# A two-layer decoder on one core: the expert mixture of a batch moves half an iteration forward

## The reference

```python
h = silu(einsum('td,eid->eti', xt, W1)) * einsum('td,eid->eti', xt, W3)
y = einsum('etd,te->td', einsum('eti,edi->etd', h, W2), combine)
```

## Time and profile before

| | us |
|---|---|
| median of 3 runs | 695.19 (691.85 to 702.54) |
| the profiled execution, its own time | 692.92 |
| its span | 691.0 |
| PE busy in the span | 538.9 (78%) |
| DVE busy | 412.9 (60%) |
| ACT busy | 298.5 (43%) |
| POOL busy | 124.3 (18%) |

### The profile page before, as it was taken

One profiled execution on the slowest core, in us unless ns is written; L12 is line 12 of the kernel. 1 busy time (PEld: TensorE's weight loads), 2 busy tenths in 40 slices (PEclk: granted clock), 3 DMA queues, 4 the chain that ended last, 5 costly groups with the idle time before them and its releaser, 6 DMA issues.

```text
span 691.0 us, 10909 instructions
## 1 busy us (share of the span) xinstructions
PE 538.9 (78%) x4385; PEld 379.9 (55%) x4412; DVE 412.9 (60%) x993; ACT 298.5 (43%) x470; POOL 124.3 (18%) x162
## 2 busy tenths in 40 slices
PE   2566627737999898998989999899998957846765
PEld 1323414415677575776767778677775734524433
DVE  3567794785446754457555573436644583573786
ACT  2314314605671136621377214763158617622443
POOL 2246052430000320000023000220003000211343
PEclk9977866967999899999999999999999997986989
DMA  6035011301000010000001000010020000000000
GB/s 212 0 142 216 25 48 48 96 9 52 1 1 2 0 62 1 2 1 1 0 2 62 1 1 1 1 63 1 1 87 6 1 0 1 1 1 0 16 16 31
DMA packets 5405, 20.98 MB, mean 30 GB/s; under 512 B 843, under 2 KB 3019, under 8 KB 4460
## 3 DMA queue, kind: packets, MB, share of 16 engines
q1 hardware_dynamic: 5356, 20.30, 8.4%
HBM read 19.25 MB, written 1.05 MB: 29 GB/s over the span
## 4 chain that ended last, share of the span: by engine, by line
PE 59%; DVE 27%; ACT 7%; issue 5%; DMA 1%; POOL 0%; SPq 0%; ACTq 0%; DVEq 0%
PE ps L872 18%; PE ps L903 16%; PE ps L652 4%; DVE nmx L1606 4%; ACT L1303 2%; PE ps L762 2%; PE ps L882 2%; PE ps L674 2%; PE ps L743 2%; PE ps L735 2%; DVE y L1503 1%; PE ps L707 1%; PE ps L634 1%; PE ps L702 1%; ACT hs L1303 1%
## 5 line engine op out<-in xcount | busy, mean ns | idle before, releaser
L1715 DVE TENSOR_TENSOR hs<-hs,ps 128x512 f32<-128x512 f32 (+1 forms) x68 | 45.6, 670 | 104.8 <-PE ps L872 58.5
L903 PE MATMUL ps<-w2f,hs 128*128 128x256 f32 x400 | 99.2, 391 | 0.0
L1303 ACT ACTIVATE hs<-ps 128x512 f32<-128x512 f32 (+1 forms) x68 | 39.7, 584 | 117.3 <-PE ps L872 116.9
L903 PEld LDWEIGHTS ps<-w2f,hs 128*128 128x128 f32 x400 | 72.0, 189 | 17.6 <-issue 9.3
L504 POOL TENSOR_TENSOR ve<-mv,half 128x2 f32<-128x2 f32 x24 | 4.7, 196 | 389.1 <-DVE mv L1496 389.1
L1606 DVE TENSOR_REDUCE nmx<-ps 128x2 f32<-128x512 f32 (+1 forms) x96 | 61.1, 681 | 9.0 <-PE ps L707 8.7
L1262 ACT ACTIVATE pk<-ps 128x512 f32<-128x512 f32 x64 | 34.7, 595 | 22.7 <-PE ps L746 22.4
L1303 ACT ACT_TABLE_LOAD x33 | 42.3, 1283 | 0.6
L872 PE MATMUL ps<-yah,w3h 128*128 128x256 f16 x200 | 38.9, 277 | 1.8 <-DVE hs L1721 1.7
L1262 ACT ACT_TABLE_LOAD x31 | 39.8, 1283 | 0.6
L872 PE MATMUL ps<-yah,w1h 128*128 128x256 f16 x200 | 39.3, 279 | 0.5 <-DVE hs L1715 0.2
(11 more groups left out here) (232 smaller groups left out, 1164.5 us busy)
## 6 DMA issues: line engine op xcount, KB each, us to landing
stage<-in_w SPq DMA_DIRECT2D x8, 800.0 KB, 4.3
tstage<-in_tern SPq DMA_DIRECT2D x4, 1024.0 KB, 4.7
w2f<-in_w SPq DMA_DIRECT2D x1, 3200.0 KB, 12.9
cs<-in_ctxT SPq DMA_DIRECT2D x1, 1024.0 KB, 10.4
cd<-in_ctxT SPq DMA_DIRECT2D x1, 1024.0 KB, 4.8
out_x<-xs SPq DMA_DIRECT2D x4, 256.0 KB, 2.2
w0s<-in_w SPq DMA_DIRECT2D x1, 768.0 KB, 7.1
xs<-in_x SPq DMA_DIRECT2D x1, 768.0 KB, 8.5
```

The costliest lines, as they stand in the source:

```text
L903: mm = pe.matmul(ps[:, bank, j * D:(j + 1) * D], hs[:, n % 4, par * S + j * P:par * S + (j + 1) * P], w, start=(first and par == 0 and j = ...
L1303: act.activation(hs[:, n % 4, 0:w], ps[:, gate_bank(n), 0:w], ACT.Silu).then_inc(e_sil.sem, 1)
L1715: TT(hs[:, n % 4, 0:w], hs[:, n % 4, 0:w], ps[:, up_bank(n), 0:w], ALU.mult).then_inc(e_hb.sem, 1)
```

## The change

The table becomes `PLACED`. Batch b's pairs fill places 7 to 12 of iteration b + 1 and 0 to 6 of iteration b + 2. The hash pairs of batch 0 fill places 9 to 12 of iteration 5; those of batch 1 places 0 to 3 of iteration 6; batches 2 and 3 stay where they were. With it go:

- `router_experts` moves from DVE's second half into its first, between the two copies of the keys; `router_turned` moves on PE and ACT to the start of the second half;
- `experts_added` and the moments of the norm behind it move from the end of an iteration into its second half (`mixture_added`);
- the score units of iteration 2, computed in iteration 1, now all use banks 2 and 3;
- the eight weight slices pass through three stage buffers in turn, ACT's and POOL's slices move forward, and PE's wait for all of them stands before iteration 1's second half;
- new waits: the first spread of a batch for `cw_ok`, the very first gate for the last exponentials of iteration 1.

```diff
-MIXED = {it: (MOE_PAIRS * (it - 2), MOE_PAIRS) for it in range(2, 2 + B)}
-MIXED[6] = (ALL_MOE, 2 * HASH_PAIRS)
-MIXED[7] = (ALL_MOE + 2 * HASH_PAIRS, HASH_PAIRS)
-MIXED[8] = (ALL_MOE + 3 * HASH_PAIRS, HASH_PAIRS)
+PLACES = 13
+SECOND_HALF = 7
+PLACED = {divmod(PLACES * (b + 1) + SECOND_HALF + p, PLACES): MOE_PAIRS * b + p
+          for b in range(B) for p in range(MOE_PAIRS)}
+for b, (it, k) in enumerate(((B + 1, 9), (B + 2, 0), (B + 3, 0), (ITS, 0))):
+    PLACED.update({(it, k + p): ALL_MOE + HASH_PAIRS * b + p for p in range(HASH_PAIRS)})
...
 def max_bank(it, n):
-    return 2 if is_mixed(it - 1) else MAX_BANKS[n % 3]
+    return 2 if is_mixed(it) else MAX_BANKS[n % 3]
...
-            for b in range(B):
-                if b == 1:
+            for q in range(2 * B):
+                b, n = divmod(q, 2)
+                if q == 3:
                     sp.dma_start(w2f[:, :], w2).then_inc(d_w2.sem, 16)
-                for n, w in enumerate((w1, w3)):
-                    if b:
-                        sp.wait_ge(wst_lo.sem, wst_lo.at(b - 1, n + 1))
-                    sp.dma_start(stage[:, n, :], w[:, b * W_SLICE:(b + 1) * W_SLICE]).then_inc(d_wst[n].sem, 16)
+                if q >= 3:
+                    sp.wait_ge(wst_lo.sem, q - 2)
+                sp.dma_start(stage[:, q % 3, :], (w1, w3)[n][:, b * W_SLICE:(b + 1) * W_SLICE]).then_inc(d_wst[q % 3].sem, 16)
...
             rsqrt_ln("context", 0)
-            rsqrt_ln("head", 2)
             split_lo(1, 0)
             split_lo(1, 1)
+            rsqrt_ln("head", 2)
+            split_lo(2, 0)
             rsqrt_ln("router", 0)
-            for n in range(2):
-                split_lo(2, n)
+            split_lo(2, 1)
             split_lo(3, 0)
+            split_lo(3, 1)
             rsqrt_ln("context", 1)
             rsqrt_ln("head", 3)
-            split_lo(3, 1)
...
-                if is_mixed(it - 1):
+                if is_mixed(it):
                     if n == 0:
-                        pe.wait_ge(p_ok.sem, p_ok.at(it - 1, 12))
+                        pe.wait_ge(p_ok.sem, p_ok.at(it - 1, 12 if is_mixed(it - 1) else 10))
...
             def router_turned(it):
                 pe.wait_ge(ctk_ok.sem, it)
-                if not is_mixed(it):
-                    pe.wait_ge(mx_ok.sem, mx_ok.at(it + 1, 12))
+                pe.wait_ge(o_ok.sem, o_ok.at(it, 2))
...
                 pe.wait_ge(e_sil.sem, n + 1)
+                if p == 0:
+                    pe.wait_ge(cw_ok.sem, b + 1)
...
             for it in range(B):
-                if it == 2:
+                phase_a(it)
+                if it == 1:
                     pe.wait_ge(wst_lo.sem, 2 * B)
                     pe.wait_ge(d_w2.sem, 16)
                     pe.wait_ge(d_sel.sem, 32)
-                phase_a(it)
                 phase_b0(it)
...
+            def mixture_added(it):
+                if 2 <= it < 2 + B:
+                    experts_added(it - 2)
+                if 2 <= it < ITS - 2:
+                    moments_of("head", it + 2)
...
                 turned_keys(it + 1, 0)
+                if routes:
+                    router_experts(it - 1)
                 own(it, 4)
...
                 maximum(it + 1, 3)
+                mixture_added(it)
                 normalised("context", b)
...
                 moments_of("tail", b)
+                mixture_added(it)
                 maximum(it + 1, 4)
```

More of the change, by code:

```diff
@@ L343, in decoder @@
         d_sel = sig("d_sel")
-        d_wst = [sig(f"d_w{n}", 16) for n in (1, 3)]
+        d_wst = [sig(f"d_wst{n}", 16) for n in range(3)]
         d_ts = sig("d_ts", 16)
@@ L909, in gates @@
             def gates(it, k):
-                if k < MIXED.get(it, (0, 0))[1]:
-                    gate(MIXED[it][0] + k)
+                n = pair_at(it, k)
+                if n is not None:
+                    gate(n)
             def ups(it, k):
-                if k < MIXED.get(it, (0, 0))[1]:
-                    up(MIXED[it][0] + k)
+                n = pair_at(it, k)
+                if n is not None:
+                    up(n)
             def outs(it, k):
-                first, count = MIXED.get(it, (0, 0))
-                if k < count:
-                    spread(first + k)
-                if 0 < k <= count:
-                    down(first + k - 1)
+                n, older = pair_at(it, k), pair_at(it, k - 1)
+                if n is not None:
+                    spread(n)
+                if older is not None:
+                    down(older)
             def gate_up(t, c):
@@ L1305, in sil @@
             def sil(it, k):
-                if k < MIXED.get(it, (0, 0))[1]:
-                    silu_of(MIXED[it][0] + k)
+                n = pair_at(it, k)
+                if n is not None:
+                    silu_of(n)
             def rounded_turned(b):
@@ L1345, in phase_a @@
                     first_turn(it + 1)
+                if it == 1:
+                    slices(2, 1)
                 if routes:
@@ L1352, in phase_a @@
                 if it < 2:
-                    slices(2 * it, 0)
+                    slices(3 * it, 0)
                 sil(it, 2)
@@ L1359, in phase_a @@
                 if it < 2:
-                    slices(2 * it, 1)
+                    slices(3 * it, 1)
                 sil(it, 3)
@@ L1382, in phase_b0 @@
                 split_hi("output", it, yTh[:, :, :])
-                if it < 2:
-                    slices(2 * it + 1, 0 if it == 0 else 1)
+                if it:
+                    router_turned(it - 1)
+                if it == 0:
+                    slices(1, 0)
+                    slices(1, 1)
                 sil(it, 8)
@@ L1738, in hb @@
             def hb(it, k):
-                if k < MIXED.get(it, (0, 0))[1]:
-                    times_up(MIXED[it][0] + k)
+                n = pair_at(it, k)
+                if n is not None:
+                    times_up(n)
             def hc(it, k):
-                if MIXED.get(it, (ALL_MOE, 0))[0] < ALL_MOE and k < MIXED[it][1]:
-                    times_share(MIXED[it][0] + k)
+                n = pair_at(it, k)
+                if n is not None and n < ALL_MOE:
+                    times_share(n)
             def own(it, k):
-                first, count = MIXED.get(it, (0, 0))
-                if first >= ALL_MOE and 0 < k <= count:
-                    own_added(first + k - 1)
+                older = pair_at(it, k - 1)
+                if older is not None and older >= ALL_MOE:
+                    own_added(older)
             def experts_added(b):
@@ L1882, in ending @@
                 own(it, 12)
-                if 2 <= it < 2 + B:
-                    experts_added(it - 2)
-                if 2 <= it < ITS - 2:
-                    moments_of("head", it + 2)
+                own(it, 13)
                 if it == ITS - 2:
@@ L1923, in phase_b0 @@
                 link(last)
-                if b:
-                    router_experts(b - 1)
                 hb(it, 9)
@@ L1970, in phase_b1 @@
                 own(it, 8)
-                if b == 0:
-                    router_experts(it - 1)
                 hb(it, 9)
```

30 lines of the change are left out of this document (16 added, 14 removed).

## The result

The changed kernel takes **710.29 us** (median of 4 runs, 708.73 to 714.46) beside 696.61 for the kernel before on the same chip: ratio **1.0229, 95% interval 1.015 to 1.0308**. A second set gave 710.71 (6 runs) beside 698.54, 1.0183 (1.0135 to 1.0231). So it is slower by 1.8 to 2.3%, some 12 to 14 us; whether by more than 2% these runs leave open. The ratios are of the executions within 1.5% of the fastest of their kernel, so they differ a little from the quotients of the medians. The forecast was 697, the range 683 to 709: the result lies 1 us outside, where rival 2 ended.

A forecast was written before the change was run, and what follows sets the result against it. Stretches last as long as PE's work or the attention chain; the change moves PE work and removes none. Terms sum to +2.6 on the profiled 692.9, giving 695.5; with the median 2.3 higher it named 697 us, range 683 to 709.

The forecast's parts named there:

- rival 2: PE's clock falls to 1.2 GHz in iteration 1's new work and behind waits in iterations 2 and 3: 707 to 709; chance 0.12.
- iteration 0, second half: POOL's slices now run beside DVE's context chain: +3.5 there, -1.6 at `mtok` and `y`, together +1.9 us.
- iteration 1: Second half takes six expert pairs into PE's idle, 38.6 us of work plus 1.7 for half clock: +17.6 us.
- iteration 2, first half: One-tile pair leaves, -1.4 us; PE busy beforehand lifts the half-clock stretch at its start, -2.5 us.
- second halves of 2 and 3: Mixture addition ahead of the context norm lengthens PE's wait, together +2.8 us; the one-tile pair moves in, +1.4 each.
- first halves of 3, 4, 5: The one-tile pair moves from the second half to the first: -1.4 us for each first half.
- iteration 4, second half: One-tile pair adds +1.4 us; the mixture addition sits where PE waits for nothing and costs 0.
- iteration 5, second half: Gives up six mixture pairs for four hash pairs, 28.1 us and 0.6 latency against 36.5: -7.8 us.
- iteration 6, first / second half: Four hash pairs leave: first half -4.5 us of a possible 0 to -7.8; second half, paced by DVE, -3.5 us.
- two clock terms: Half clock at the start of iteration 1's filled half, +1.7 us; less half clock at iteration 2's start, -2.5 us.
- Rivals 3 and 4: Late slices hold PE before iteration 1's second half; hash downs wait for their weights' DMA (`cd`): 700 each, chance 0.05 each.
- Rival 1: PE's idle in iteration 5's second half and iteration 6 does not reopen: 13 us off, 682.5 to 685; chance 0.20.

The follow-up runs named there:

- fillers in both kernels: Matmuls that compute nothing put ahead of turns PE waits for, up to iteration 6: changed kernel 703.9 us, kernel before 693.76 us.
- the filled pairs: Changed kernel and kernel before, both with matmuls that compute nothing: up to iteration 6, 703.9 and 693.76 us; in the tail too, changed orders mended, 695.87 and 687.04.
- mending the order: Changed kernel with GpSimd's norms for head 2 and the router put ahead of the weight slices in iteration 0: 709.26 us.
- the last pair: Compute-nothing matmuls up to and in the tail: changed kernel with GpSimd's norms and the last ternary slice reordered 695.87 us, kernel before 687.04 us.
- the two mended orders: Changed kernel with GpSimd's norms ahead of iteration 0's slices (alone 709.26 us), and the last ternary slice behind iteration 6's first silus (alone 713.53 us).

## Why the prediction was wrong

| term | forecast | measured, first execution |
|---|---|---|
| iteration 0, second half | +1.9 | +5.2 |
| iteration 1 | +17.6 | +18.4 |
| iteration 2, first half | -3.9 | -2.1 |
| second halves of 2 and 3 | +5.6 | +4.5 |
| first halves of 3, 4, 5 | -4.2 | -0.3 |
| iteration 4, second half | +1.4 | +4.4 |
| iteration 5, second half | -7.8 | -6.7 |
| iteration 6, first / second half | -4.5 / -3.5 | -0.8 / -2.0 |
| elsewhere (start, iteration 7, tail) | 0 | +1.2 |
| sum | +2.6 | +21.8 |

The sum is that of the two profiled executions, some 8 us more than the medians' difference of 13.7.

1. **The step that failed is the clock.** The forecast carried two clock terms, +1.7 in iteration 1 and -2.5 in iteration 2, -0.8 together, and priced all the rest as at full clock. PE's busy time grew by 19.5 and 14.7 instead. What that cost is shown for iterations 2 to 6: they gave back 3.0 to 3.3 us of the 16.9, and 9.4 with fillers in both kernels.
   It is not the whole miss. Without clock terms the forecast is +3.4 in all and -14.4 for iterations 2 to 6; the filled pairs have +12.1 and +6.8, and -9.4 and -10.5. PE's idle seemed to bear the account out, +2.2 and +2.7 without fillers for +3.4, but part of the waits was then covered by slow work: in the filled pairs PE's time without real work grew by 4.4 (with 7.6 more of busy time) and by 9.0.
2. **Rival 2 was right in kind and wrong in place.** It was given 0.12, and the medians, 710.3 and 710.7, lie just above its 707 to 709. It looked for slow work in iteration 1, whose second half held its clock, and for one stretch in iterations 2 and 3, which came. It did not look where work is taken away. The argument against it, "iteration 3's equal wait cost no clock", rested on one execution, and waits of one length do not cost alike: the 1.9 us wait for `qh` in iteration 3's first half had a low stretch behind it in the changed kernel (284.7) and none before, and none with eight fillers one half earlier.
3. **Iteration 1**: size and mechanism right (40.0 us against 38.6 + 1.7). The other 1.8 of the +18.4 is iteration 1's first half.
4. **Iteration 0**: the mechanism (DVE's steps pass slowly beside GpSimd's pieces) held, +4.4 instead of +3.5 in the chain. The forecast let eight steps pass beside eight pieces and took 3.8 us as their time alone; that is the time of ten (88.83 to 92.62 before), and ten passed, in 8.2 us (88.39 to 96.58). As for the rest, the 1.6 expected back at `mtok` and `y` was 0.8 + 1.3 = 2.1 (1.02 and 0.73 us after, for the earlier trace rows's 1.82 and 2.02). The remaining 2.9 of the +5.2 stand beside a clock of 0.57 in that half, 0.75 before. The second execution has about 4 us more than before in that half, and mending the order took 3.5 of them. The Trainium skill ("SBUF — State Buffer", Who interferes with whom) has the shared port locked by two-input steps and fast scalar ones, never by reductions: the rows agree for `am` (0.69) and for `cf` (1.38), and the reciprocal kept its 0.17.
5. **Iteration 6** (-2.8 for -8.0): the ternary slice cost `y` 2.8 us, which no step named, though it is the contention of iteration 0 again; moving it gave back only 1.1, since PE then waited for ScalarE. The rest stands beside a low clock (0.87 and 0.58); how it splits is not shown.
6. **Iteration 4**: the move let a down wait for `xm_ok`, 1.70 us. The forecast said that the same DVE steps come before it is due; here they don't. It cost the wait and a stretch at low clock.
7. **First halves of 3, 4 and 5** (-0.3 for -4.2): here the clock is not the cause, those of 4 and 5 ran at 1.00 before and after and got 0.4 and 0.6 us shorter, not 1.4 each. Gates and ups gave 0.9 us of PE's time in each; what took the rest back is open.
8. Rivals 3 and 4 did not occur: POOL's last slice ended at 129.7, 11 us before it was due, and the hash downs were not held by `cd`. Rival 1 fell: idle from iteration 5's second half to 6's end went from 12.2 to 22.5 us, as forecast ("some 25").

The forecast's own sum gives 695.5 + 2.3 = 697.8, not the 697 that it names; that decides nothing here.

**Open.** What decides whether a wait of some 2 us costs clock; how the 9.0 us of waits in the last pair split between the move and the two mended orders; and why the iteration-7-and-tail stretch, the same work in both kernels, took 3.0 to 3.3 us more in the changed one in two pairs of kernels and nothing in a third (122.2 and 121.9). The kernel before shows both: 117.9 us at clock 0.86 as it is, 122.2 at 0.79 with fillers that end in iteration 6.

## What to carry to other kernels

Work moved from a full stretch into an idle one also moves the idle, and here PE's clock fell where it came to lie: price what is left behind at the low level, not only the hole that is filled. A slow engine also covers its own waits, so equal idle does not say that the waits are equal: fill them in both kernels, then compare. Before moving real work to keep PE busy, try matmuls that compute nothing ahead of the turns it waits for: here they took some 9 us, 1.3%, off the tuned kernel (687.0), and the move added 12 to 14. And when two steps on VectorE and GpSimd change places in time, look for what else meets: one ternary slice on one 0.73 us step cost 2.8 us, and moved away it held up ScalarE and cost PE a wait of 1.5 to 3.0.

## What the runs showed that was not expected

- Executions of one kernel on one core differ by up to 10 us with the granted clock (702.8 at 0.899, 712.5 at 0.879). The kernel before with fillers spreads over 3 to 4 us, the changed one with them over 5 to 8.
- The clock fell behind waits as short as 1.70 us (431.11). The same wait of 1.70 us stands in the filled kernels (424.90 with fillers everywhere), and no low stretch follows it.
- Two VectorE instructions of 0.73 us together took 3.56 beside GpSimd's `tensor_scalar` steps of 1.9, 1.4 us more for each: less than one GpSimd instruction.
